# Cross attention with a top-2 expert layer on one core: straight dense half, fixed blank rows, q as products of heads and rests

## The chip, the cores and the metric

The kernel runs on one core of one Trainium2 chip. The metric is device time in microseconds (us) of one launch, the median of the runs; lower is better. The core has five engines that run side by side, each through its own list of instructions in order: PE (TensorE: matmuls and weight loads), DVE (VectorE), ACT (ScalarE), POOL (GpSimd) and SP (SyncE, here only a queue that starts DMAs). They wait for each other by semaphores.

## What is computed

64 batches of 256 tokens with 256 features, and for each batch a context of 120 rows:

```
h   = layernorm(x)
q   = h @ Wq.T + bq ;  k, v = ctx @ Wk.T + bk, ctx @ Wv.T + bv      (16 heads of 16)
att = (q @ (k.T @ v) per head) * 0.25                               (no softmax)
x1  = x + layer_norm(att + h, gamma, beta)
t   = layernorm(x1);  logits = t @ gate.T;  w, e = top2(softmax(logits))   (16 experts)
out = x1 + sum over the two choices of w * relu(t @ expert_w[e].T + expert_b[e])
```

## The kernel before

**The dense half** goes over the 64 batches in steps. In step `s` the engines work on four batches at once: batch `s` (transposes of h, k and v, q, k.T v), `p = s - 1` (attention and its residual, x1), `b = s - 2` (norm and transposes of x1, logits) and `f = s - 3` (top 2, ranks, scatter of the rows). The order on each engine is written by hand in its `step(s)`, and the engines meet through semaphores named after what is ready (`s_ht`: h transposed and copied, `s_oh`: one-hot marks ready, `s_prk`: ranks ready, `s_x1`: x1 ready). Steps up to `LEAD - 1 = 11` are written out, then a loop on every engine runs 6 times over 8 steps, and the last steps are written out again.

On PE a step is: attention of p (L673), four transposes of h (L687), k and v as three products of heads and rests (L661 to L663: a head is a value rounded to the type fp32r, a rest is what the rounding left), the first half of q (L707, plain fp32), the ranks of f (L734), transposes of x1 (L717), k.T v (L695), the second half of q (L707), logits (L729). On DVE it is: moments of x1 of b, scores of f, moments of the next x, top values (L1050), their indices (L1060), gaps (L1055, L1056), the indices cast to floats (L1067), the attention residual `att` (L1111), one-hot marks (L1071), moments of att, a shift for the next h (L1038), the ranks picked (L1096, which waits for L734), then scaling, the mask of k.T v, the softmax weights, the place of each row and x1 (L1137). POOL waits for x1 of p and then does the rest of the next context (L579), x + beta (L594), in steps 4 to 11 the rest of one eighth of the expert weights (L602), small integer work, and two scatters of 128 rows into `bins` (L621). In steps 2 to 9 PE also sums the columns of an eighth of the expert weights (L765, L767: one bf16 and two fp32 matmuls of 512 columns), and DVE folds the sum in a step later (L1150).

`settle` puts a semaphore increment of its own between a wait and the next instruction:

```
def settle(eng, passed):
    eng.sem_inc(passed, 1)
```

**The boundary.** When the last ranks are counted (`s_end`), the number of rows of every expert is known. DVE works out a table of row positions (L1231 to L1273), PE transposes it between matmuls that nobody reads (`keep_warm`, 12 ahead of the transpose and 14 behind it, L798), and `fill` (L378) writes for each of 16 experts 128 blank rows behind the expert's last row, by DMAs from DRAM to DRAM (L386): 8 started by SP, 8 by ACT. SP then reads 16 row positions into registers and starts the loads of the first rows (L488), after waiting for those DMAs (`s_padw`).

**The expert half** goes twice (first and second choice) over 144 tiles of 128 rows: load by SP, transpose by PE (L811), head by ACT (L982), rest by DVE (L1277), three products of 256 columns (L828 to L830), weighing by ACT, sum by DVE, scatter by POOL (L636). PE reads the offsets of the expert weights into registers at the top of each `multiply` (L835).

## Time and profile before

| | |
|---|---|
| time, median of 3 runs | 903.47 us (901.72 to 903.67) |
| profiled execution, own time | 903.09 us |
| its span in the trace | 901.3 us |
| PE busy | 769.8 us, 85% of the span |
| DVE busy | 664.3 us, 74% |
| ACT busy | 612.0 us, 68% |
| POOL busy | 582.3 us, 65% |

How to read it: the shares are means over stages with different limits. The dense half takes roughly the first 480 us, the boundary some 20, the expert half the rest. The span is what the trace covers; the execution's own time is 1.8 us longer.

### The profile page before, as it was taken

To read this page: it belongs to the slowest core of one execution; us is meant where nothing else is said; L and a number is where in the kernel's file an instruction comes from. 1 tells how busy PE (TensorE), PEld (TensorE's weight loads), DVE (VectorE), ACT (ScalarE), POOL (GpSimd) and SP (SyncE) were. 2 spreads that over 40 slices of the span, in tenths; PEclk is the share of its full clock that TensorE was granted. 3 is DMA by queue.
4 is the path that set the end of the run, shared out by engine and by line. 5 is a ranking of instruction groups with operands and counts; after the bars stand their busy time and mean duration, and the time that the engine had idled before them with its cause. 6 is when DMAs were issued, how large, how long until landed. Compare 5 with 4: busy or idle time off the path is not lost.

```text
span 901.3 us, 22390 instructions
## 1 busy us (share of the span) xinstructions
PE 769.8 (85%) x5549; PEld 676.3 (75%) x5550; DVE 664.3 (74%) x2291; ACT 612.0 (68%) x1722; POOL 582.3 (65%) x704
## 2 busy tenths in 40 slices
PE   4999999999999999999975878777777899777760
PEld 3777788888888888888863867677765899776760
DVE  4788999999999999999983767676763566455540
ACT  3788889999999999999970545455552565455440
POOL 3267766666666666666662577777775577777775
PEclk9999999999999999999996899999999899999995
DMA  6425556666665666666515799989985999999942
GB/s 205 153 82 160 159 180 203 219 228 200 223 228 196 231 218 200 230 215 205 190 49 169 234 306 302 307 282 311 309 295 203 323 392 352 302 290 292 310 168 76
DMA packets 138485, 207.27 MB, mean 230 GB/s; under 512 B 39718, under 2 KB 75049, under 8 KB 138185
## 3 DMA queue, kind: packets, MB, share of 16 engines
q1 hardware_dynamic: 113740, 131.56, 46.7%
q0 software_dynamic: 24448, 74.14, 22.0%
q10 hardware_dynamic: 256, 1.08, 0.4%
q8 instruction: 18, 0.29, 0.1%
q14 instruction: 23, 0.19, 0.1%
HBM read 89.91 MB, written 118.97 MB: 232 GB/s over the span
## 4 chain that ended last, share of the span: by engine, by line
PE 53%; DMA 14%; issue 12%; POOL 9%; DVE 5%; SPq 4%; ACT 1%; POOLq 0%; DVEq 0%; ACTq 0%
PE ps_q L707 12%; PE ps_att L673 7%; POOL out_rows L636 6%; PE ps_mg L729 5%; DMA row_in<-bins 5%; DMA bins<-row_in,put_at 4%; PE ps_mg L695 4%; DMA out_rows<-xh,put_at 3%; PE ps_h2t L717 3%; PE ps_kv L661 3%; PE ps_kv L663 3%; PE ps_kv L662 3%; PE ps_ht L687 3%; POOL bins L636 3%; SPq L495 2%
## 5 line engine op out<-in xcount | busy, mean ns | idle before, releaser
L636 POOL DMA_INDIRECT bins<-row_in,put_at x143 | 141.5, 990 | 68.1 <-issue 38.8
L636 POOL DMA_INDIRECT out_rows<-xh,put_at x143 | 145.0, 1014 | 56.6 <-issue 38.4
L621 POOL DMA_INDIRECT bins<-rows x128 | 128.0, 1000 | 75.9 <-POOL rows L614 50.3
L707 PE MATMUL ps_q<-h_t,wq 128*128 128x256 f32 x512 | 132.3, 381 | 0.0
L579 POOL TENSOR_TENSOR c_rest<-c_sb,c_head 128x240 fp32r<-128x240 f32 x64 | 44.3, 692 | 106.2 <-DVE x L1137 102.6
L707 PEld LDWEIGHTS ps_q<-h_t,wq 128*128 128x128 f32 x512 | 92.5, 191 | 15.5 <-ACT h_t L934 0.4
L828 PE MATMUL ps_q<-we_head,row_head 128*128 x288 | 88.4, 307 | 9.7 <-DVE row_rest L1277 9.7
L1304 DVE SCALAR_TENSOR_TENSOR row_in<-row_in 128x256 f32<-128x256 f32 x144 | 63.4, 481 | 33.8 <-ACT row_in L994 32.4
L594 POOL TENSOR_TENSOR x_beta<-xh,beta_sb 128x512 f32<-128x512 f32 x64 | 81.9, 1279 | 1.2 <-DVE x L1137 1.2
L830 PE MATMUL ps_q<-we,row_head 128*128 x288 | 81.7, 284 | 0.0
L829 PE MATMUL ps_q<-we_head,row_rest 128*128 x288 | 81.6, 283 | 0.0
L729 PEld LDWEIGHTS ps_mg<-wg_centred,h_t 128*128 128x128 f32 x512 | 64.3, 194 | 13.5 <-issue 4.9
L887 ACT ACTIVATE q_t<-ps_q,bq_sb 128x256 f32<-128x256 f32 x128 | 60.3, 471 | 20.0 <-PE ps_q L707 20.0
L673 PE MATMUL ps_att<-kvm,q_t 128*128 128x128 f32 x512 | 72.9, 285 | 0.8 <-ACT q_t L887 0.8
L1308 DVE COPY put_at<-row_in 128x2 int32<-128x2 int32 x72 | 14.3, 198 | 78.3 <-ACT xh L994 78.3
L926 ACT ACTIVATE xh<-xh,nmr,rstd 128x256 f32<-128x256 f32 x128 | 69.1, 588 | 0.2 <-DVE nmr L1038 0.2
L874 ACT ACTIVATE lnv<-st,eps 128x2 f32<-128x2 f32 x192 | 54.5, 284 | 15.2 <-DVE st L1032 15.2
L729 PE MATMUL ps_mg<-wg_centred,h_t 128*128 128x16 f32 x512 | 63.4, 256 | 1.6 <-ACT h_t L940 1.6
L828 PEld LDWEIGHTS ps_q<-we_head,row_head 128*128 128x128 f32 x288 | 55.1, 191 | 12.6 <-issue 12.5
L673 PEld LDWEIGHTS ps_att<-kvm,q_t 128*128 128x128 f32 x512 | 62.3, 192 | 1.4 <-ACT q_t L887 1.3
L911 ACT ACTIVATE rows<-x,rows 128x256 f32<-128x256 f32 x128 | 58.1, 501 | 2.1
L661 PE MATMUL ps_kv<-wkv_head,c_head 128*120 128x512 f32 x128 | 56.1, 438 | 4.0 <-DMA bkv_rows<-bkv_dram 3.8
(179 smaller groups left out, 2436.4 us busy)
## 6 DMA issues: line engine op xcount, KB each, us to landing
bins<-zeros SPq DMA_DIRECT2D x48, 768.0 KB, 4.5
row_in<-bins SPq DMA_DIRECT2D x128, 260.0 KB
row_in<-bins SPq DMA_DIRECT2D x160, 132.0 KB
xh<-in_x SPq DMA_DIRECT2D x64, 256.0 KB
c_sb<-in_ctx_t SPq DMA_DIRECT2D x64, 120.0 KB
we<-in_we_t SPq DMA_DIRECT2D x8, 512.0 KB, 6.3
bins<-row_in,put_at POOLq DMA_INDIRECT x143, 4.1
out_rows<-xh,put_at POOLq DMA_INDIRECT x143, 4.5
```

The costliest lines, as they stand in the source:

```text
L594: pool.tensor_tensor(x_beta[:, n], x_sb[:, s.buf(4)], beta_sb[:].unsqueeze(1).to_broadcast([P, NT, D]), ALU.add).then_inc(s_xb, 1)
L621: pool.indirect_dma_start(out=bins[0], in_=r[:, t, :], out_offset=bass.IndirectOffsetOnAxis(ap=r[:, t, POS_COL:POS_COL + 1].bitcast(I32), ...
L636: pool.indirect_dma_start(out=bins[1] if k == 0 else out, in_=row_in[:, t, :] if k == 0 else y[:, t, :], out_offset=bass.IndirectOffsetOnA ...
L661: pe.matmul(ps_kv[0:SC, :], head, wkv_head[:, c, :], start=(c == 0), stop=False)
L673: mm = pe.matmul(ps_att[:, t, c * P:(c + 1) * P], q_t[:, c, t, :], kvm[:, c, :], start=True, stop=True)
L707: mm = pe.matmul(ps_q[dc][:, 0:S], wq[:, c, dc * P:(dc + 1) * P], h_t[:, c, :, :], start=(c == 0), stop=(c == KC - 1))
L729: mm = pe.matmul(logits[:, t, :], h2_t[:, c, t, :], wg_centred[:, c, :], start=(c == 0), stop=(c == KC - 1))
L828: pe.matmul(o, heads, w_head, start=(c == 0), stop=False)
L829: pe.matmul(o, rests, w_head, start=False, stop=False)
L830: mm = pe.matmul(o, heads, we_rest[:, c, bass.ds(at[2 * j + t], D)], start=False, stop=(c == KC - 1))
L926: a = act.activation(h[:, b.buf(4), t, :], x_sb[:, b.buf(4), t, :], ACT.Identity, bias=nmr[:, t:t + 1], scale=rstd[:, 0, b.buf(2), t:t + 1])
L1304: at = dve.scalar_tensor_tensor(out=row_in[:, t, 0:D], in0=row_in[:, t, D:2 * D], scalar=row_in[:, t, D + S_COL:D + S_COL + 1], in1=row_in ...
```

## The change

1. **Straight code.** The loops of the dense half are written out on all engines; `Batch` loses its loop index.
2. **Fixed blank rows.** Every region of `bins[0]` keeps 128 rows at each end, which are filled with blanks in step 7 (four DMAs in place of the two that wrote `pad_rows`). An expert's rows begin behind them, and the table counts tiles so that the blank rows at the start of a region fill its last tile. `fill`, its DMAs and `pad_at` are gone. SP reads the first 4 positions ahead of the first loads and the other 12 after two pairs; PE reads its first offsets ahead of the first transposes.
3. **q in three products.** `wq` and `h` are split in heads and rests. ACT's copy of the transposed h writes `h_head`; DVE makes `h_rest` (new, 128x512 from PSUM and SBUF) between the attention residual and the one-hot marks; both halves of q and the next transposes of h wait for it (`s_hr`).
4. **Small work on DVE.** The two subtractions of the gaps are one; the one-hot marks read the integer indices; the cast of the second index goes to POOL. `settle` is gone from the dense half.
5. **Column sums.** POOL adds the two halves of an eighth of the expert weights (`we_sum`, 128x512) in steps 1 to 8, and PE sums columns with one fp32 matmul in place of two.
6. `WARM_TABLE` 12 to 16, `WARM_LOADS` 14 to 20.

```diff
-                for c in range(KC):
-                    mm = pe.matmul(ps_q[dc][:, 0:S], wq[:, c, dc * P:(dc + 1) * P], h_t[:, c, :, :],
-                                   start=(c == 0), stop=(c == KC - 1))
+                o, part = ps_q[dc][:, 0:S], slice(dc * P, (dc + 1) * P)
+                for c in range(KC):
+                    pe.matmul(o, wq_head[:, c, part], h_head[:, c, :, :], start=(c == 0), stop=False)
+                    pe.matmul(o, wq_head[:, c, part], h_rest[:, c, :, :], start=False, stop=False)
+                    mm = pe.matmul(o, wq_rest[:, c, part], h_head[:, c, :, :], start=False, stop=(c == KC - 1))
...
+            def rest_h(b):
+                dve.wait_ge(s_ht, b.times(1, 1))
+                dve.tensor_tensor(h_rest[:], ps_ht[:], h_head[:].bitcast(F32), ALU.subtract).then_inc(s_hr, 1)
...
+                    for n in pieces(s.c - 1, 1):
+                        pool.wait_ge(s_we[n], 16)
+                        if n >= 2:
+                            pool.wait_ge(s_wsum, n - 1)
+                        pool.tensor_tensor(we_sum[:, n % 2], we[:, 0, piece(n)], we[:, 1, piece(n)],
+                                           ALU.add).then_inc(s_whalf, 1)
...
-                for c in range(KC):
-                    mm = pe.matmul(ps_fold, minus_ones[:], we[:, c, piece(n)], start=False, stop=(c == KC - 1))
-                mm.then_inc(s_wsum, 1)
+                pe.matmul(ps_fold, minus_ones[:], we_sum[:, n % 2], start=False, stop=True).then_inc(s_wsum, 1)
...
-                dve.tensor_tensor(gaps[:, :, 0:E], scores[:], top[:, :, 0:1].to_broadcast([P, NT, E]), ALU.subtract)
-                dve.tensor_tensor(gaps[:, :, E], top[:, :, 1], top[:, :, 0], ALU.subtract).then_inc(s_gap, 1)
+                dve.tensor_tensor(gaps[:], scores_top[:, :, 0:E + 2], top[:, :, 0:1].to_broadcast([P, NT, E + 2]),
+                                  ALU.subtract).then_inc(s_gap, 1)
...
+                    regions = bins[0][0:SPARE, :].rearrange("(r n) d -> n r d", n=REGION)
+                    facts = pad_facts[:, 0].rearrange("p (r o) d -> p r o d", o=2)
+                    for o, ends in enumerate((regions[0:PAD], regions[REGION - PAD:REGION])):
...
-            fill(sp, 0, E // 2)
             for n in range(4):
                 sp.wait_ge(s_row[n], 32 * (NB // 4))
+            sp.wait_ge(s_init, 2 * 16 * (E // 4 + 2))
             sp.wait_ge(s_table, 1)
```

On DVE, in the middle of any step of the dense half, the program before has these rows (words in brackets are the semaphores that a row waits for):

```order
L1060 MAX_INDEX top_i<-top,scores 128x8
L1055 TENSOR_TENSOR gaps<-scores,top 128x2x16 [waits top_values_ready]
L1056 TENSOR_TENSOR gaps<-top 128x2
L1067 CAST rows<-top_i 128x2x2 [waits rows_scattered3,top_indices_ready]
L1111 TENSOR_TENSOR att<-ps_att,xh 128x512 [waits h_ready,attention_multiplied]
L1071 TENSOR_TENSOR onehot<-iota_e,rows 128x64 [waits indices_as_floats]
L1032 BN_STATS st<-att 128x6 [waits attention_residual_ready]
```

And in the changed program, at the same place:

```order
L1052 MAX_INDEX top_i<-scores_top 128x8
L1045 TENSOR_TENSOR gaps<-scores_top 128x36 [waits top_values_ready]
L1099 TENSOR_TENSOR att<-ps_att,xh 128x512 [waits h_ready,attention_multiplied]
L1103 TENSOR_TENSOR h_rest<-ps_ht,h_head 128x512 [waits h_t_heads_ready]
L1057 TENSOR_TENSOR onehot<-iota_e,top_i 128x64 [waits top_indices_ready]
L1022 BN_STATS st<-att 128x6 [waits attention_residual_ready]
```

A row of 2 elements and a cast are gone, and a subtraction of 512 elements stands between the residual and the marks. On PE, behind the products for k and v of the same step, before:

```order
L664 MATMUL ps_kv<-bkv_rows,ones_bf 120x512
L705 REGISTER_ALU [waits h_t_copied]
L707 MATMUL ps_q<-h_t,wq 128x256 [waits q_copied]
L707 MATMUL ps_q<-h_t,wq 128x256
L734 MATMUL ps_rank<-onehot,not_before 128x32 [waits rank_picked,onehot_ready]
```

and in the changed program:

```order
L653 MATMUL ps_kv<-bkv_rows,ones_bf 120x512
L697 MATMUL ps_q<-h_head,wq_head 128x256 [waits q_copied,h_t_rests_ready]
L698 MATMUL ps_q<-h_rest,wq_head 128x256
L699 MATMUL ps_q<-h_head,wq_rest 128x256
L697 MATMUL ps_q<-h_head,wq_head 128x256
L698 MATMUL ps_q<-h_rest,wq_head 128x256
L699 MATMUL ps_q<-h_head,wq_rest 128x256
L725 MATMUL ps_rank<-onehot,not_before 128x32 [waits rank_picked,onehot_ready]
```

The ranks still stand behind this half of q, which now waits for DVE's `h_rest` and not for ACT's copy. On POOL, in one of steps 4 to 8, before:

```order
L594 TENSOR_TENSOR x_beta<-xh,beta_sb 128x512 [waits x_loaded1]
L602 TENSOR_TENSOR we<-we,we_head 128x2x512 [waits weight_heads_ready]
L614 TENSOR_TENSOR rows<-rows,exps 128x2 [waits first_weight_ready]
```

and in the changed program:

```order
L574 TENSOR_TENSOR x_beta<-xh,beta_sb 128x512 [waits x_loaded3]
L584 TENSOR_TENSOR we_sum<-we 128x512 [waits weight_column_sums_ready,expert_weights_loaded6]
L589 TENSOR_TENSOR we<-we,we_head 128x2x512 [waits weight_heads_ready]
L598 TENSOR_TENSOR rows<-rows,id_step 128x2 [waits rows_scattered0]
L600 CAST rows<-top_i 128x2 [waits top_indices_ready]
L603 TENSOR_TENSOR rows<-rows,exps 128x2 [waits first_weight_ready]
```

A second large addition stands ahead of the rest of the expert weights, and a cast among the small rows.

## Rows read from the trace of the kernel before

**Rows 1.** Busy time in 100 us of the dense half, and its heading.
```profile
core 0: us, PE busy (x) PEld busy (x) DVE busy (x) ACT busy (x) POOL busy (x), PEclk, DMA share, GB/s
300.00:400.00 100.00, 100.00 (x730) 87.96 (x727) 94.66 (x390) 93.63 (x298) 62.53 (x90) 1.00 0.64 217
```

**Rows 2.** Timeline of PE in one step: start, length, engine, line.
```profile
305.61 1.03 PE L707 MATMUL ps_q<-h_t,wq 128*128 128x256 f32 x4
306.47 0.18 PE L734 MATMUL ps_rank<-onehot,not_before 128*128 128x32 bf16 x1
...
306.60 0.18 PE L734 MATMUL ps_rank<-onehot,before 128*128 128x32 bf16 x1
...
309.29 1.14 PE L673 MATMUL ps_att<-kvm,q_t 128*128 128x128 f32 x8
```

**Rows 3.** Timeline of DVE in the same step; idle time before a row in brackets.
```profile
304.47 0.09 DVE L1060 MATCH_VALUE_LOAD top_i<-top,scores 128x8 f32 x1 [0.15 <-DVE top L1050]
...
304.78 0.17 DVE L1055 TENSOR_TENSOR gaps<-scores,top 128x32 f32<-128x32 f32 x1
304.87 0.19 DVE L1056 TENSOR_TENSOR gaps<-top 128x2 f32<-128x2 f32 x1
304.98 0.15 DVE L1067 CAST rows<-top_i 128x4 f32<-128x4 uint32 x1
305.05 0.68 DVE L1111 TENSOR_TENSOR att<-ps_att,xh 128x512 f32<-128x512 f32 x1
305.65 0.21 DVE L1071 TENSOR_TENSOR onehot<-iota_e,rows 128x64 bf16<-128x64 f32 x1
...
306.81 0.23 DVE L1096 TENSOR_TENSOR picked<-ps_rank,onehot 128x64 f32<-128x64 f32 x1
```

**Rows 4.** Timeline of PE in the expert half: products of heads and rests, 256 columns.
```profile
500.19 0.28 PE L830 MATMUL ps_q<-we,row_head 128*128 x1
500.31 0.29 PE L828 MATMUL ps_q<-we_head,row_head 128*128 x1
```

**Rows 5.** Timeline of PE: the transposes of h that begin steps 9, 10, 11, 12, 63.
```profile
89.36 0.60 PE L687 MATMUL ps_ht<-ident,xh 128*128 128x128 f32 x4
...
98.16 0.60 PE L687 MATMUL ps_ht<-ident,xh 128*128 128x128 f32 x4
...
105.02 0.60 PE L687 MATMUL ps_ht<-ident,xh 128*128 128x128 f32 x4
...
113.59 0.60 PE L687 MATMUL ps_ht<-ident,xh 128*128 128x128 f32 x4
...
458.48 0.60 PE L687 MATMUL ps_ht<-ident,xh 128*128 128x128 f32 x4
```

**Rows 6.** Timelines of POOL (its step 10) and DVE (its step 11).
```profile
104.91 1.29 POOL L594 TENSOR_TENSOR x_beta<-xh,beta_sb 128x512 f32<-128x512 f32 x1
106.16 2.36 POOL L602 TENSOR_TENSOR we<-we,we_head 128x1024 fp32r<-128x1024 f32 x1
...
106.23 2.34 DVE L1055 TENSOR_TENSOR gaps<-scores,top 128x32 f32<-128x32 f32 x1
```

**Rows 7.** The boundary: timelines of PE, POOL, SP's queue and DVE.
```profile
479.09 4.58 PE L798 MATMUL ps_q<-bkv_rows,ones_bf 128*128 128x512 bf16 x12
...
481.71 0.96 POOL L621 DMA_INDIRECT bins<-rows  x1 [0.30 <-issue]
...
484.08 0.28 DVE L1273 CAST table<-ps_kv 8x128 int32<-8x128 f32 x1 [0.36 <-PE ps_kv L803]
...
490.62 8.94 SPq L488 DMA_DIRECT2D row_in<-bins  x16
...
493.46 1.09 PE L811 MATMUL ps_ht<-ident,row_in 128*128 128x128 f32 x4 [6.46 <-DMA row_in<-bins]
```

**Rows 8.** The chain that ended last, at the boundary: the blank rows.
```profile
486.29 4.16 DMA bins<-pad_rows
```

**Rows 9.** Timelines of the first product and the first scatter of the expert half.
```profile
496.41 0.58 PE L828 MATMUL ps_att<-we_head,row_head 128*128 x1 [0.79 <-DVE row_rest L1277]
...
501.94 0.95 POOL L636 DMA_INDIRECT bins<-row_in,put_at  x1 [19.27 <-DVE row_in L1304]
```

More of the change, by code:

```diff
@@ L94, in settle, with dense_steps @@
     eng.sem_inc(passed, 1)
-def dense_steps(eng, step, low, high):
-    for s in range(low, LEAD):
-        step(Batch(None, s))
-    with eng.Fori(0, LOOPS) as i:
-        for j in range(U):
-            step(Batch(i, LEAD + j))
-    for s in range(LEAD + LOOPS * U, high):
-        step(Batch(None, s))
+def dense_steps(step, low, high):
+    for s in range(low, high):
+        step(Batch(s))
 def expert_bodies(eng, body, k, peel_first=0, peel_last=0):
@@ L135, in table_reader, with read @@
     regs = [eng.alloc_register(f"column{column}_{n}") for n in range(V)]
-    def read(k, i):
+    def read(k, i, count=V):
         half = int(isinstance(i, int) and i * V >= P)
         row = (column * 2 + k) * 2 + half
-        eng.load(regs, table[row:row + 1, bass.ds(i * V - half * P, V)])
-        return [nc.snap(r, min_val=0, max_val=max_val) for r in regs]
+        low = V - count if count > V // 2 else 0
+        eng.load(regs[low:low + count], table[row:row + 1, bass.ds(i * V - half * P + low, count)])
+        return [nc.snap(r, min_val=0, max_val=max_val) for r in regs[low:low + count]]
     return read
@@ L397, in load @@
                 n = b.buf(4)
-                if b.i is not None or b.c >= 4:
+                if b.c >= 4:
                     sp.wait_ge(s_xb, (b - 4).times(1, 1))
@@ L465, in step @@
                     load(nxt)
-                if s.i is None and s.c < LEAD:
+                if s.c < LEAD:
                     prepare_experts(s.c)
-                if s.i is not None:
-                    fill_second(s, s.c - LEAD)
-            dense_steps(sp, step, 0, NB)
-            fill(sp, 0, E // 2)
+                if LEAD <= s.c < LEAD + FILLS:
+                    fill_second(s.c - LEAD)
+            dense_steps(step, 0, NB)
             for n in range(4):
                 sp.wait_ge(s_row[n], 32 * (NB // 4))
+            sp.wait_ge(s_init, 2 * 16 * (E // 4 + 2))
             sp.wait_ge(s_table, 1)
@@ L678, in transpose_h @@
                 pe.wait_ge(s_h, b.times(1, 1))
-                if b.i is not None or b.c >= 1:
-                    pe.wait_ge(s_ht, (b - 1).times(1, 1))
-                if b.i is None and b.c >= 2:
+                if b.c >= 1:
+                    pe.wait_ge(s_hr, (b - 1).times(1, 1))
+                if b.c >= 2:
                     pe.wait_ge(s_gfold, 1)
-                if b.i is None and b.c >= 3:
+                if b.c >= 3:
                     pe.wait_ge(s_fold, min(b.c - 2, WE_PIECES))
@@ L746, in rank_tokens @@
                 pe.wait_ge(s_oh, b.times(1, 1))
-                if b.i is not None or b.c >= 1:
+                if b.c >= 1:
                     close_ranks(b - 1)
@@ L834, in multiply @@
             def multiply(k, i):
-                at = offsets(k, i)
+                at = first_at if isinstance(i, int) and i == 0 else offsets(k, i)
                 for j in range(PAIRS):
@@ L848, in _ @@
                     keep_warm(ps_rank, WARM_BOUNDARY)
+                first_at = offsets(k, 0)
                 for j in range(2):
@@ L882, in copy_q @@
                 act.wait_ge(s_pq, b.times(2, dc + 1))
-                if dc == 0 and (b.i is not None or b.c >= 1):
+                if dc == 0 and (b.c >= 1):
                     act.wait_ge(s_patt, (b - 1).times(1, 1))
-                if b.i is None and b.c == 0:
+                if b.c == 0:
                     act.wait_ge(s_w[2], 32)
@@ L967, in step @@
                     context_head(s + 2)
-                for n in pieces(s.c - 3, 1) if s.i is None and s.c >= 3 else ():
+                for n in pieces(s.c - 3, 1):
                     act.wait_ge(s_fold, n + 1)
                     act.activation(we_head[:, :, piece(n)], we[:, :, piece(n)], ACT.Copy).then_inc(s_whead, 1)
-            dense_steps(act, step, -1, NB + 3)
-            fill(act, E // 2, E)
+            dense_steps(step, -1, NB + 3)
             def head_rows(k, i, j):
@@ L1204, in step @@
                     first_weights(f)
-                if f.i is None and f.c == NB - 1:
+                if f.c == NB - 1:
                     second_weights(f)
@@ L1213, in _ @@
             split(be_in[:], be_rest, be_part, 5)
-            dense_steps(dve, step, -1, NB + 3)
+            dense_steps(step, -1, NB + 3)
             steps = [0]
```

244 lines of the change are left out of this document (114 added, 130 removed).

## The prediction

> **What bounds the kernel now.** I read the stages first, then one step of the dense half on each engine, then the steps one after another, then the boundary. In the dense half PE has no idle time and DVE is busy 94.66% [rows 1]. One step of PE, from one product to the same one in the next, takes 6.70 us, and half of q takes 0.86 of it (305.61 to 306.47) [rows 2]. So PE sets the pace, but DVE is close behind: of 6.70 us it works 6.34. It idles 0.15 ahead of the index search, and it waits for the ranks: the last one ends at 306.60 + 0.18 = 306.78, and DVE picks them at 306.81 [rows 2, 3]. Hence two questions: what does PE save, and what does the work given to DVE cost there?
>
> The steps are not all alike. Step 9 takes 8.80 us (89.36 to 98.16), as the steps with column sums do, step 10 takes 6.86, and step 11 takes 8.57 without any column sum [rows 5]. There is a reason on DVE: a subtraction of 32 elements (L1055) that takes 0.17 us elsewhere takes 2.34 here, started 0.07 us behind POOL's rest of the expert weights (L602, 2.36 us), and ends with it [rows 3, 6]. An operation of DVE with both inputs in SBUF stands still while POOL works on two inputs. There is a second such hold one step later.
>
> At the boundary the table is ready at 484.36, but the first loads of rows start at 490.62, behind the blank rows, whose last DMA lands at 486.29 + 4.16 = 490.45 [rows 7, 8]. The first transposes follow at 493.46 and the first scatter of the expert half at 501.94 [rows 7, 9].
>
> **q in three products.** On PE a half of q becomes six products of 256 columns. Products of that shape start 0.12 us apart [rows 4]: 0.72 in place of 0.86, 0.28 less over a step. PE's own turn falls to about 6.42.
>
> On DVE `h_rest` is new: 512 elements, one input from PSUM and one from SBUF, like the attention residual in front of it, which takes 0.68 and lets the next one start after 0.60 [rows 3]. Taken out are the second gap subtraction (0.11, 304.87 to 304.98), the cast (0.07, 304.98 to 305.05), and with `settle` most of the 0.15 of idle time; I take 0.11 for that, an estimate, since a same-engine wait stays [rows 3]. If nothing made DVE wait, its turn would be 6.65 to 6.76 (6.34 + 0.60 less 0.18 to 0.29).
>
> But it does wait, and this is the step on which the forecast rests. Half of q on PE now waits for `h_rest`, the ranks stand behind this half, and DVE picks the ranks only three operations after it has made `h_rest` (marks, moments, shift: 1.43 us from the start of `h_rest` if nothing waits, by the spacing of the same rows now). From the start of the residual to the pick it takes 1.76 us now (305.05 to 306.81). After: 0.60 for the residual, 0.68 for `h_rest`, 0.05 for the semaphore, 0.72 for half of q, 0.31 for the ranks (306.47 to 306.78), 0.03 to the pick: 2.39 [rows 2 to 4]. The rest of DVE's turn is 6.70 - 1.76 = 4.94, less 0.29 = 4.65. The turn that closes over both engines is 7.04 us: DVE stands about 0.4 in front of the pick, PE about 0.65 in front of q. Against 6.70 that is 0.34 a step. Bounds: 6.95 if the semaphores and the first product are quicker by 0.1, 7.15 if `settle` was not what cost the 0.15. Over the 50 steps from 13 on: +17.0.
>
> **Straight code.** From step 10 to step 63 it is 360.3 us [rows 5]. Steps 10, 11 and 12 take 6.86, 8.57 and as much again for the second hold; 50 steps at 6.70 are 335.0, which leaves about 1.4 us for all ends of the loop. That is what writing it out gives: -1.4. So the long steps around the loop's entry are not the loop's. Straight steps show no stall: steps 2 to 9 are straight now and run alike. The Trainium skill says more ("Runtime: NRT & Kernel Launch", section on instruction fetch mechanics): a taken branch whose target is not at hand costs a fetch, and fetching straight code is hidden; by it the straight program costs nothing, and the traces of the straight steps agree.
>
> **Column sums, the early steps.** PE loses one of two fp32 matmuls of 512 columns, as many columns as the 0.86 of half a q: -0.86 in steps 2 to 9 [rows 2]. The pace there then goes to DVE (7.04 and the fold of more than 1 us, about 8.4) and to POOL: 62.5% of 6.70 is 4.2, with L602 6.5, with the new addition (the shape of x + beta, 1.29) 7.8, and with the idle time around its scatters close to 9.1 [rows 1, 6]. The new addition also moves L602 back by 1.25 us, onto the moment when DVE comes to its gap subtraction, and by my reckoning from these rows the two are within 0.03 us. If DVE comes first, five steps take 9.1 in place of 8.8, and with what steps 2 to 5 gain it is -1 in all. If POOL comes first, DVE is held some 2.2 us in each of five steps, which take 10.6: +9, and +7 in all. It is a tie; I put +3 in the sum and both ends in the range.
>
> The skill speaks against this part ("GPSIMD Engine Reference", Specifications): GpSimd shares its SBUF interfaces with VectorE and contends with its instructions that have two SBUF inputs. The 2.34 us of row L1055 agree; `h_rest`, with one input from PSUM, would be free of it, and the kernel's order keeps POOL's big additions behind x1.
>
> **The end of the dense half and the start.** The last three steps are chains of short operations; the cast, the gap and `settle` are on them: -0.5. At the start q follows the first k and v as now; -0.3 for its quicker products.
>
> **The boundary.** No blank rows stand ahead of the loads. What is late next is the table. Four more matmuls ahead of its transpose: the 12 took 4.58 together, 0.38 each; four of 512 columns at twice the 0.12 of 256 are about 0.9 [rows 4, 7]. That puts the table at 485.3. The last scatter is issued by 482.67 [rows 7] and should be down by about 485 to 486.8 (the blank rows took 4.16 among many [rows 8]). With 1 us for SP to read four positions the loads start at about 486.2, 4.4 earlier. PE stays at work until then, where now it idles 6.46 us ahead of the first transposes [rows 7] and does them and the first products at the lower clock, up to twice the 0.12 each. It also has its offsets already; now the first product starts 0.79 after the transposes [rows 9]. From the first transpose to the first scatter it is 8.48 us now; 12 products at the full clock give up to 1.2 of it, the transposes and the offsets as much: -2.3, an estimate. Together -6.7, with bounds -3 (the last scatter lands late, POOL sets the pace anyway) and -8. The expert half behind it is the same code, its pace set by POOL's scatters and the DMAs, so it moves as a whole.
>
> **The sum.** 903.1 for the profiled execution (0.4 below the median), -0.3 at the start, +3 in the early steps, +17.0 - 1.4 in the rest, -0.5 at the end, -6.7 at the boundary: 914.2, as a median 914.5 us.
>
> **Rivals.**
> - *DVE hides the new work.* It idles already, and the pick waits at present for PE alone. If the turn over both engines is not closed as I have it, DVE's own 6.65 to 6.76 is the step; then 50 steps give -2.5 to +3, and with -1 early, -1.4, -0.8 and -6.7 the time is 891 to 897. For it: the other rows of DVE's turn leave no other wait. Against it: `h_rest`, half of q, ranks and pick follow each other by semaphores in both programs' order. It turns the sign below a step of 6.82 to 6.90. Chance 0.12 for faster; 0.06 that the turn falls between and all is within 0.2%.
> - *The boundary gives little:* the loads wait for the last scatter or the table, and POOL's scatters take back what comes early. Then -3 or less: 918 to 921. Chance 0.07.
> - *Straight code stalls an engine:* every engine now fetches several times the instructions. A stall of 2 us every few steps makes 922 and more. No straight step shows one. Chance 0.05.
> - *The forecast,* with its own range of 907 to 920: 0.70.
>
> Faster, same and slower by 0.2% (1.8 us, about what a measurement tells from no change): 0.12, 0.06, 0.82. The range leaves out the first rival below 902 and what lies above 921.
>
> **What the profile after would show.** The transposes of h 7.04 us apart, even in steps 20 to 60; PE idle or late in front of L697 on DVE's `h_rest`, DVE idle some 0.4 in front of the ranks picked, PE's busy share below 95%. Early steps of 10.6 with the gap subtraction at 2 us, or of 9.1 without. The first loads at about 4.4 us closer behind the table, and full clock there. The prediction is wrong if steps are 6.8 or less, if many rows of DVE or PE show stalls of 2 us, or if the boundary is as long as before.

## The result and the profile after

The kernel before took 902.6 us (901.3 to 903.7, 4 runs), the changed one 923.1 us (918.3 to 925.6, 4 runs): a ratio of 1.022, 95% interval 1.018 to 1.027. It is slower, as forecast, but by 20.5 us in place of 11, and above my range (902 to 921). The profiled execution of the changed kernel took 925.58 us with a span of 923.6, so it lies 2.5 above its median.

Busy time in the same 100 us of the dense half as [rows 1]:

```profile
core 0: us, PE busy (x) PEld busy (x) DVE busy (x) ACT busy (x) POOL busy (x), PEclk, DMA share, GB/s
300.00:400.00 100.00, 95.52 (x743) 82.45 (x742) 93.66 (x351) 91.93 (x282) 60.62 (x98) 1.00 0.63 206
```

PE, which had no idle time, now has 4.5%, and no other engine is busier than before: nobody is full. That is what a turn that closes over two engines looks like. The groups of the page say where PE idles:

```profile
L697 PE MATMUL ps_q<-h_head,wq_head 128*128 128x256 f32 x256 | 85.1, 332 | 29.6 <-DVE h_rest L1103 29.6
```

The same step as [rows 2, 3], DVE first, then PE (start, length, engine, line, idle time before it):

```profile
305.63 0.24 DVE L1040 MAX8 scores_top<-scores_top 128x8 f32<-128x16 f32 x2
305.90 0.09 DVE L1052 MATCH_VALUE_LOAD top_i<-scores_top 128x8 f32 x1
...
306.21 0.18 DVE L1045 TENSOR_TENSOR gaps<-scores_top 128x36 f32<-128x36 f32 x1
306.30 0.68 DVE L1099 TENSOR_TENSOR att<-ps_att,xh 128x512 f32<-128x512 f32 x1
306.90 0.68 DVE L1103 TENSOR_TENSOR h_rest<-ps_ht,h_head 128x512 fp32r<-128x512 f32 x1
307.50 0.24 DVE L1057 TENSOR_TENSOR onehot<-iota_e,top_i 128x64 bf16<-128x64 f32 x1
...
308.80 0.23 DVE L1082 TENSOR_TENSOR picked<-ps_rank,onehot 128x64 f32<-128x64 f32 x1 [0.37 <-PE ps_rank L725]
```

```profile
307.63 0.38 PE L697 MATMUL ps_q<-h_head,wq_head 128*128 128x256 f32 x1 [0.32 <-DVE h_rest L1103]
307.86 0.28 PE L698 MATMUL ps_q<-h_rest,wq_head 128*128 128x256 f32 x1
307.97 0.28 PE L699 MATMUL ps_q<-h_head,wq_rest 128*128 128x256 f32 x1
...
308.44 0.19 PE L725 MATMUL ps_rank<-onehot,not_before 128*128 128x32 bf16 x1
...
308.58 0.18 PE L725 MATMUL ps_rank<-onehot,before 128*128 128x32 bf16 x1
```

PE waits 0.32 for the rests, DVE waits 0.37 for the ranks, each for the other once a turn. From the residual to the pick it is 2.50 us (306.30 to 308.80), where I had 2.39. The piece that I mis-sized is the first product of the six: the next one follows it by 0.23 (307.63 to 307.86), the others stand 0.11 to 0.13 apart. It isn't the wait that makes it so. The second half of q, ahead of which PE has no idle time, begins nearly alike (timeline of PE):

```profile
309.44 0.37 PE L697 MATMUL ps_q<-h_head,wq_head 128*128 128x256 f32 x1
309.65 0.28 PE L698 MATMUL ps_q<-h_rest,wq_head 128*128 128x256 f32 x1
```

The steps, by the transposes of h (steps 10, 13 and 63; the first row answers to 98.16 of [rows 5]):

```profile
99.65 0.60 PE L676 MATMUL ps_ht<-ident,xh 128*128 128x128 f32 x4
...
126.61 0.60 PE L676 MATMUL ps_ht<-ident,xh 128*128 128x128 f32 x4
...
483.69 0.60 PE L676 MATMUL ps_ht<-ident,xh 128*128 128x128 f32 x4
```

From 126.61 to 483.69 there are 50 steps of 7.14. Steps 2 to 12 are 7.7 to 8.96 long, but for two: step 9 takes 12.77 and step 12 takes 11.10. In the first of them (POOL, then DVE):

```profile
87.71 1.29 POOL L584 TENSOR_TENSOR we_sum<-we 128x512 f32<-128x512 f32 x1
88.95 2.34 POOL L589 TENSOR_TENSOR we<-we,we_head 128x1024 fp32r<-128x1024 f32 x1
```

```profile
88.25 0.17 DVE L1052 FIND_INDEX8 top_i<-scores_top 128x8 uint32<-128x16 f32 x1
88.34 3.06 DVE L1045 TENSOR_TENSOR gaps<-scores_top 128x36 f32<-128x36 f32 x1
91.32 0.68 DVE L1099 TENSOR_TENSOR att<-ps_att,xh 128x512 f32<-128x512 f32 x1
```

An operation of 0.18 us takes 3.06: it meets POOL's addition (L584) and stands through the rest of the weights (L589) as well. I call this a hold. In the early steps of 8.96 us it stands only for the end of L584, gets in ahead of L589 and takes 0.43 or less; there it is the one-hot marks, also from SBUF to SBUF, that stand until L589 ends, for 1.22 in place of 0.24 (step 8; L589 from 79.73 to 82.08):

```profile
80.94 1.22 DVE L1057 TENSOR_TENSOR onehot<-iota_e,top_i 128x64 bf16<-128x64 f32 x1
```

The hold of step 9 makes DVE only 1.9 us later than a step of 8.96 (3.06 less 0.18, less the 1.0 that the marks no longer stand). The other 1.9 is PE's: it idles 3.56 ahead of q, and then runs at half the clock. The window behind the wait (its clock is the 0.50 near the end of the line):

```profile
93.10:96.30 3.20, 3.20 (x22) 3.11 (x21) 1.78 (x7) 1.47 (x4) 1.36 (x2) 0.50 0.26 90
```

The variant with the rests of h ahead of the attention has the same hold. In the third set of experiments below its clock stayed up:

```profile
90.40:93.00 2.60, 2.10 (x22) 2.06 (x23) 2.60 (x8) 0.94 (x4) 1.52 (x4) 1.00 0.31 69
```

In the second set it fell:

```profile
92.60:97.00 4.40, 4.40 (x25) 4.31 (x26) 3.24 (x13) 1.49 (x5) 1.97 (x2) 0.50 0.30 83
```

Where the clock falls to 0.50 (1.2 GHz), DVE waits for PE's ranks, k.T v and column sum.

The boundary, beside [rows 7, 9]: PE, DVE, SP's queue, PE, POOL.

```profile
503.85 6.39 PE L787 MATMUL ps_q<-bkv_rows,ones_bf 128*128 128x512 bf16 x16
...
510.45 0.28 DVE L1259 CAST table<-ps_kv 8x128 int32<-8x128 f32 x1 [2.23 <-PE ps_kv L792]
...
514.52 0.66 PE L800 MATMUL ps_ht<-ident,row_in 128*128 128x128 f32 x4
...
520.98 0.97 POOL L625 DMA_INDIRECT bins<-row_in,put_at  x1 [13.56 <-DVE row_in L1290]
```

```profile
511.65 9.59 SPq L468 DMA_DIRECT2D row_in<-bins  x16
```

The last pick of ranks ends at 503.69 (478.94 before). From there to the table it is 6.76 us (5.14 before), to the first loads 7.96 (11.68), to the first scatter 17.29 (23.00). The loads come 3.7 earlier, and the way from the first transposes to the first scatter is 6.46 in place of 8.48. The clock of both sides of the table, by windows:

```profile
503.90:509.30 5.40, 5.40 (x16) 1.86 (x14) 3.84 (x27) 0.00 (x0) 1.96 (x2) 0.50 0.14 50
510.50:514.00 3.50, 3.50 (x18) 1.55 (x16) 0.23 (x1) 0.00 (x0) 0.00 (x0) 1.00 0.28 79
```

The 16 matmuls ahead of the table run at a granted clock of 0.50 (1.2 GHz), after a tail in which PE was busy for 4.2 of 7.7 us (496.0 to 503.7) at that clock already, and stand 0.43 apart; the 20 behind it run at 1.00 and stand 0.22 apart.

Where the 22.3 us between the two spans lie: -0.8 at the start, +5.3 in steps 1 to 13, +20.7 in steps 13 to 63, -0.5 from there to the last pick, -5.7 to the first scatter, and +3.3 in the expert half. The last is the same code, and it takes 394.8 to 401.9 us in the profiles of the last three sets of experiments, 402.6 here and 399.4 in the kernel before: spread between executions, by all that these show.

### The profile page after: what moved, and what is told of

The parts are those of the page before. It is cut to its first block, busy times and chain, and to the rows that moved or that the text cites. A ratio compares the mean times of both kernels' runs of the same rounds, so it can differ in the third digit from the quotient of the medians.

```text
span 923.6 us, 21777 instructions
## 1 busy us (share of the span) xinstructions
PE 772.2 (84%) x5799; PEld 679.6 (74%) x5800; DVE 693.7 (75%) x2225; ACT 626.5 (68%) x1723; POOL 602.7 (65%) x776
## 4 chain that ended last, share of the span: by engine, by line
DVE 35%; issue 22%; PE 17%; DMA 10%; POOL 9%; SPq 4%; ACT 2%; DVEq 0%; POOLq 0%; ACTq 0%
POOL out_rows L625 6%; DVE x L1129 6%; DVE scaled L1116 5%; DVE h_rest L1103 4%; DMA bins<-row_in,put_at 4%; DVE att L1099 4%; DMA row_in<-bins 4%; POOL bins L625 3%; DVE st L1022 3%; PE ps_q L697 3%; DVE top_i L1052 2%; DMA out_rows<-xh,put_at 2%; DVE scores_top L1040 2%; SPq L475 2%; DVE gaps L1045 1%
## 5 line engine op out<-in xcount | busy, mean ns | idle before, releaser
L625 POOL DMA_INDIRECT bins<-row_in,put_at x143 | 143.5, 1004 | 62.9 <-issue 38.6
L697 PE MATMUL ps_q<-h_head,wq_head 128*128 128x256 f32 x256 | 85.1, 332 | 29.6 <-DVE h_rest L1103 29.6
L697 PEld LDWEIGHTS ps_q<-h_head,wq_head 128*128 128x128 f32 x256 | 49.2, 192 | 59.4 <-DVE h_rest L1103 59.1
L698 PE MATMUL ps_q<-h_rest,wq_head 128*128 128x256 f32 x256 | 72.4, 283 | 0.0
L699 PE MATMUL ps_q<-h_head,wq_rest 128*128 128x256 f32 x256 | 72.2, 282 | 0.0
L879 ACT ACTIVATE q_t<-ps_q,bq_sb 128x256 f32<-128x256 f32 x128 | 60.4, 472 | 13.5 <-PE ps_q L699 13.5
L720 PE MATMUL ps_mg<-wg_centred,h_t 128*128 128x16 f32 x512 | 67.4, 264 | 1.5 <-ACT h_t L932 1.4
```

Of the source, the lines that this page charges most:

```text
L625: pool.indirect_dma_start(out=bins[1] if k == 0 else out, in_=row_in[:, t, :] if k == 0 else y[:, t, :], out_offset=bass.IndirectOffsetOnA ...
L697: pe.matmul(o, wq_head[:, c, part], h_head[:, c, :, :], start=(c == 0), stop=False)
L698: pe.matmul(o, wq_head[:, c, part], h_rest[:, c, :, :], start=False, stop=False)
L699: mm = pe.matmul(o, wq_rest[:, c, part], h_head[:, c, :, :], start=False, stop=(c == KC - 1))
L720: mm = pe.matmul(logits[:, t, :], h2_t[:, c, t, :], wg_centred[:, c, :], start=(c == 0), stop=(c == KC - 1))
```

## The experiments

Edits are against the changed kernel unless said otherwise. They come in five sets. Each set had its own chip with its own runs of the kernel before, so a ratio is comparable within a set. On the chips of the first two sets the kernel before took 1056 us in place of 902, and every kernel was slower in nearly all steps from 13 on and in the expert half; absolute times in the expectations of these two sets were made for 902.

**First set.** Three variants of the changed kernel, and one of the kernel before.

`e1`: the rests of h ahead of the attention.

```diff
-                if p.exists():
-                    add_attention(p)
                 if s.exists():
...
                     rest_h(s)
+                if p.exists():
+                    add_attention(p)
```

> The changed kernel with one thing moved: DVE makes h_rest ahead of the attention residual in place of behind it. Nothing is left out. Theory A (the loss is a turn over two engines: residual 0.60, h_rest 0.68, half of q, ranks, then the pick, 7.14 us a step): h_rest comes 0.6 us earlier, the wait ahead of the pick goes, and a step falls to what DVE or PE needs by itself, 6.65 to 6.75 us. Over the 50 steps that is 19 to 25 us, and 2 to 9 more in the early steps: about 893 to 901 against 923. Theory B (DVE simply has too much work, 0.6 us more a step): the order changes nothing, the step stays at 7.1 and the time within 3 us of 923. Theory C (straight code is slow to fetch): likewise no change.

`e3`: q as before the change (`h_t`, `wq`, one fp32 product; no `h_rest`), all else of the change kept.

```diff
-                    pe.matmul(o, wq_head[:, c, part], h_head[:, c, :, :], start=(c == 0), stop=False)
-                    pe.matmul(o, wq_head[:, c, part], h_rest[:, c, :, :], start=False, stop=False)
-                    mm = pe.matmul(o, wq_rest[:, c, part], h_head[:, c, :, :], start=False, stop=(c == KC - 1))
+                    mm = pe.matmul(o, wq[:, c, part], h_t[:, c, :, :], start=(c == 0), stop=(c == KC - 1))
```

> The changed kernel with q as before: plain fp32 matmuls from one copy of h, no heads and rests of Wq and h, no h_rest on DVE. Nothing is left out. Theory A: a step falls to PE's 6.70 us, the early steps and the boundary keep their gains: 891 to 899. Theory B (too much work on DVE) says the same here. Theory C (straight code): a step stays above 7.0 us and the time above 915.

`e5`: the column sums again as two fp32 matmuls on PE, POOL's `we_sum` taken out.

> The changed kernel with the column sums as before: two fp32 matmuls on PE, no addition of the two halves on POOL. Nothing is left out. If the two gap subtractions of 3.06 and 2.86 us in the early steps come from POOL's additions in a row, at least the first of them goes and the time falls by 2 to 6 us. Rival: they belong to the rest of the expert weights alone, as the two holds of 2.3 us before did, and the early steps only get PE's 0.86 us back eight times: the time rises by 0 to 4 us.

`e4`: the kernel before, with its dense half written out straight and nothing else of the change.

> The kernel before with its dense half written out, and nothing else changed. Theory A: 1 to 2 us faster (the ends of six loops), no stalls. Theory C (fetching straight code stalls the engines): several us slower.

| kernel | us | ratio to before, 95% |
|---|---|---|
| rests first | 1046.3 | 0.992, 0.989 to 0.995 |
| q plain | 1042.2 | 0.987, 0.983 to 0.990 |
| sums on PE | 1062.5 | 1.006, 1.003 to 1.008 |
| before, straight | 1046.3 | 0.991, 0.987 to 0.994 |

The order is as the turn through the rests wants it, but the steady steps are 7.5 us and more, the straight version of before too (7.52), so this chip doesn't tell 7.14 from 6.70, and the changed kernel itself was not in this set. Straight code costs nothing: it took 9.6 us less than before, more than the 1 to 2 expected, and why so much was not found (1.8 in the third set). With the sums on PE the first of the two holds shrinks to 0.90 and the second stays (2.82), but the early steps are 9.6 to 9.7 us, where the changed kernel has 8.96 in the next set, and the ratio is 1.006 against 1.000 there. So the rival was right, and the sums on POOL are no loss.

**Second set**, to have the changed kernel itself beside its variants.

> The changed kernel unchanged, as the mark for the others of this call. 2% slower than the kernel before if this chip runs the dense half as the first one did (steps of 7.14 us against 6.70); about level with it if the steady steps are 7.5 us for both, as in the four runs before.

> h_rest ahead of the attention residual, nothing else, once more, since in the run before all steady steps stood at 7.5 us for another reason, with the mask of k.T v waiting 0.7 us each step. Theory A (turn over two engines): steps of 6.65 to 6.75 us, 893 to 901 us, 2 to 3% faster than the changed kernel. Theory B (too much work on DVE): like the changed kernel.

> q as before in the changed kernel, once more for the same reason. Theory A: steps of 6.70 us, 891 to 899 us. If a step stays above 7.0 us, q is not where the time goes.

`f4` has the rests first and `WARM_TABLE` 10 in place of 16.

> h_rest ahead of the residual, and 10 matmuls in place of 16 ahead of the transpose of the table. In the profile of the changed kernel the 16 take 6.2 us and the table's transpose waits 2 us for them. Theory: 1.5 to 2.5 us faster than the kernel with h_rest first alone. Rival: the scatter of the last rows lands no sooner, or PE's clock falls for want of work, and nothing is gained.

Measured against before: the changed kernel 1.000 (0.998 to 1.003, 1056.8 us), rests first 0.990 (0.985 to 0.995), q plain 0.988 (0.983 to 0.993), rests first with 10 matmuls 0.988 (0.983 to 0.994). So on this chip the change costs nothing, and both ways of freeing q from the wait give 1%, where 2 to 3% were expected; the 10 matmuls are not told from the 16. What made the steps long there? I put it down to the blank rows that SP writes to the second bins: one step near the end took 7.14 in the changed kernel and 6.7 in the others, and I took it for a step without them (step 62). The windows don't bear that out. It is step 60, in which the last of them are written, and the steps 61 and 62 behind it, with hardly any transfers left, are long again (the changed kernel, 500.04 is the start of step 61):

```profile
492.90:500.04 7.14, 6.82 (x55) 5.89 (x54) 6.67 (x26) 6.51 (x21) 4.23 (x7) 1.00 0.58 191
500.04:507.70 7.66, 6.77 (x55) 5.83 (x54) 6.78 (x27) 6.44 (x21) 4.45 (x9) 1.00 0.14 50
```

In the straight version of before step 62 takes 7.52 as well, at 40 GB/s. The short step 60 also has POOL's second scatter issued some 2 us later than in the steps around it; whether that matters was not tried, and in the straight version of before step 61 is short (6.81) without it. The next set was made for the theory of the blank rows.

**Third set**: three of these kernels and the straight version of before, with these blank rows written two portions a step in steps 36 to 59, so that steps 14 to 35 are without them.

```diff
-                if LEAD <= s.c < LEAD + FILLS:
-                    fill_second(s.c - LEAD)
+                half = LEAD + FILLS // 2
+                if half <= s.c < LEAD + FILLS:
+                    fill_second(2 * (s.c - half))
+                    fill_second(2 * (s.c - half) + 1)
```

> The changed kernel with the blank rows of the second bins written two portions a step in steps 36 to 59 instead of one a step in steps 12 to 59 (same bytes, same rows, same order of everything else). Steps 14 to 35 then run without those transfers. My theory (the closed turn of VectorE and TensorE through the rests of h sets the step, and the transfers only lay something on top on this chip) expects 7.14 us a step there, as in the profile of the changed kernel and in its step 62 here (7.14), instead of the 7.6 to 7.85 of the run before. The rival (the slower steps on this chip are of the chip, whatever the transfers) expects 7.6 to 7.85 there as well. For steps 36 to 59 both leave 7.8 or more; the time as a whole 1045 to 1060.

> The same late blank rows, and VectorE makes the rests of h ahead of adding the attention. My theory: with the 0.60 us of add_attention out of the turn the step is set by what set it before the change, so 6.70 to 6.75 us in steps 14 to 35, 0.4 less than the kernel with the late rows alone, about 9 us over those 22 steps and some 15 to 20 over the dense half. The rival (the turn is paced by VectorE's whole work or by PE's own, not by what stands ahead of the rests) expects 7.1 in both.

> The same late blank rows, and q as one plain fp32 product on TensorE as before the change (no heads, no rests), everything else of the change in place. My theory: 6.70 us in steps 14 to 35, as before the change and as with the rests first, so that three products of heads and rests bring nothing in a steady step even when they no longer cost: TensorE's 0.28 us a step are not on the path that sets it. The rival (a faster q shows once the wait for the rests is gone) expects this kernel 0.1 to 0.3 us a step behind the one with the rests first.

> The kernel before with its dense half written out straight and the same late blank rows (nothing else of the change): the yardstick of the other three. Both theories expect 6.69 to 6.71 us in steps 14 to 35, as in the profile of the kernel before; if it is 7.5 as with the blank rows spread over steps 12 to 59, the slower steps on this chip are not from those transfers and the comparison of the steady steps has to be made otherwise.

This chip was one like that of the prediction (before: 901.2 us, 25 runs):

| late blank rows and | us | ratio to before, 95% | steady step |
|---|---|---|---|
| nothing else | 919.3 | 1.019, 1.013 to 1.025 | 7.14 |
| rests first | 897.4 | 0.996, 0.994 to 0.999 | 6.72 |
| q plain | 894.8 | 0.994, 0.991 to 0.996 | 6.70 |
| before, straight | 899.3 | 0.998, 0.996 to 1.000 | 6.70 |

One exchange of two operations on DVE is worth 22 us (919.3 to 897.4). The rests-first kernel in steps with twice the blank rows, by windows:

```profile
290.00:430.00 140.00, 139.88 (x1104) 122.88 (x1104) 138.12 (x520) 133.27 (x418) 92.22 (x147) 1.00 1.02 334
```

At 334 GB/s the steps are as long as without the transfers (6.72), so here they lay nothing on top; what makes the steps long on the other two chips was not found. And DVE has no idle time in a steady step. From one subtraction to the next pick (rests first, timeline of DVE, a step without blank rows):

```profile
204.74 0.18 DVE L1047 TENSOR_TENSOR gaps<-scores_top 128x36 f32<-128x36 f32 x1
204.91 0.69 DVE L1105 TENSOR_TENSOR h_rest<-ps_ht,h_head 128x512 fp32r<-128x512 f32 x1
205.51 0.68 DVE L1101 TENSOR_TENSOR att<-ps_att,xh 128x512 f32<-128x512 f32 x1
...
206.92 0.22 DVE L1084 TENSOR_TENSOR picked<-ps_rank,onehot 128x64 f32<-128x64 f32 x1
```

The pick has no wait before it. 6.72 is DVE's own work, inside the 6.65 to 6.76 that I had for a DVE that never waits. With q plain it is PE's own, 6.70. So the cheaper q never shows in a steady step: what PE saves, DVE spends. And PE saves less than I had: half of q takes 0.81 with the rests first too, where the plain one takes 0.86, and PE is busy for 139.88 of the 140 us.

**Fourth set**, for the early steps and the table. `h5`: the gap subtraction as two operations with one tensor input.

```diff
-                dve.tensor_tensor(gaps[:], scores_top[:, :, 0:E + 2], top[:, :, 0:1].to_broadcast([P, NT, E + 2]),
-                                  ALU.subtract).then_inc(s_gap, 1)
+                for t in range(NT):
+                    i = dve.tensor_scalar(gaps[:, t, :], scores_top[:, t, 0:E + 2], top[:, t, 0:1], None, ALU.subtract)
+                i.then_inc(s_gap, 1)
```

> The changed kernel with one edit: VectorE's gap subtraction is two operations with one tensor input and a scalar per partition each, in place of one with two tensor inputs in SBUF. My theory (the holds of 3.06 and 2.86 us are that operation standing still while GpSimd works on two SBUF inputs): the new operations take 0.1 to 0.2 us everywhere, the two steps of 12.77 and 11.10 fall to about 9 and 8, so 6 to 8 us less over steps 1 to 13; steady steps get longer by the second operation, at most 0.1 us (7.2), or +4 us over the dense half. In all 0 to 6 us below the changed kernel (917 to 923 where that has 923). The rival (the long steps come from something else, such as GpSimd's own work, and the hold only lies in it) expects the same two long steps with the wait moved to another operation.

`h1` is the same with the rests first.

> The rests of h ahead of the attention and the gap subtraction with one SBUF tensor input. By my theory the holds (3.06 and 2.87 us in the kernel with the rests first and late blank rows) are gone and steps 9 to 12 lose some 5 us; VectorE sets the steady step with its own work (6.72, no idle time in it), so the second small operation adds its 0.08 to 0.1 to every step: 6.80 to 6.82, +5 us. In all about the time of the rests first alone, 897 to 901 where the kernel before has 901. The rival expects long steps as before and 6.8 us in the steady ones, about 904.

`h3` has q plain and `WARM_TABLE` 10; `h4` adds the one-input subtraction to it.

> q plain as before the change, and 10 matmuls ahead of the transpose of the table in place of 16. The timeline of the changed kernel shows those 16 start 0.42 us apart (at the lower clock) and the table's cast waiting 2.23 us for the transpose behind them. My theory: 6 fewer are worth 6 x 0.42 = 2.5 us, of which at most 2.2 us show before the table's own computation ends last: first loads of the expert half 2 us earlier after the last pick than in the kernel with 16, unless the last scatter has not landed. In all 893 where the kernel before has 901. The rival (the loads wait for the last scatter of the dense half, not for the table) expects the first loads at the same place, 0 us gained.

> q plain, 10 matmuls ahead of the table, and the gap subtraction with one SBUF tensor input. TensorE sets the steady step here (6.70) and VectorE has 0.5 us to spare, so the second small operation is hidden, and the holds of the gap subtraction (2.2, 1.7 and 2.9 us in the kernel with q plain) go: by my theory 3 to 6 us less than q plain with 10 matmuls, 887 to 890 where the kernel before has 901, the best of all. The rival expects no gain over q plain with 10 matmuls.

Measured, with before at 902.0 us: `h5` 944.3 (ratio 1.046, 1.042 to 1.051), `h1` 912.4 (1.012, 1.008 to 1.015), `h3` 893.4 (0.990, 0.987 to 0.994), `h4` 894.7 (0.992, 0.989 to 0.995). My expectation of the holds fell: the one-input form is held too, and more often. `h5`, timelines of POOL and DVE:

```profile
77.66 2.36 POOL L589 TENSOR_TENSOR we<-we,we_head 128x1024 fp32r<-128x1024 f32 x1
```

```profile
77.51 0.17 DVE L1053 FIND_INDEX8 top_i<-scores_top 128x8 uint32<-128x16 f32 x1
77.60 2.46 DVE L1046 TENSOR_SCALAR gaps<-scores_top 128x18 f32<-128x18 f32 x2
79.97 0.68 DVE L1100 TENSOR_TENSOR att<-ps_att,xh 128x512 f32<-128x512 f32 x1
```

The first of the two gets through, the second meets L589 at 77.66 and ends with it. Eight early steps have one of 1.2 to 2.5 us, one step takes 13.58 us, and steps 1 to 13 grow by another 13.5 us. `h1` has the steady step that was expected (6.81), and the same kind of long early steps (up to 13.03). The steady step is 7.31: the pair takes 0.27 instead of 0.09 on the path ahead of the rests, and 0.17 of these 0.18 show. In `h4`, where PE sets the steady step, the same 0.18 cost nothing (6.70). Its early steps are 9.53 in place of 8.95 in `h3`, and these 0.58 are not the price of its hold of 2.48: in `h3` the marks stand in its place (1.81 for 0.21), so DVE loses 0.6 in all. The table in `h3` is ready 5.12 us after the last pick instead of 5.95 in `g3`, and the first scatter follows 15.81 instead of 16.48 after it: 6 matmuls fewer are worth 0.7 by this, where 2 were expected: in `g3` the table waits only 1.20 for its transpose (2.23 in the changed kernel's profile), and in `h3` 0.36, so the table's own computation ends last. The two profiles are of different chips, and the times (893.4 and 894.8) don't tell the difference.

**Fifth set**: the subtraction as it is, but behind the rests of h.

```diff
                     top_indices(f)
-                    score_gaps(f)
...
                 if f.exists():
+                    score_gaps(f)
                     mark_experts(f)
```

> The changed kernel with one move: VectorE's gap subtraction stands behind the attention and the rests of h instead of ahead of them. My theory: a hold then stands behind the rests of h, TensorE goes on with q, and the attention and the rests (1.2 us) are done while GpSimd still adds: the steps of 12.77 and 11.10 fall by at least 1.2 each, to 11.5 and 9.9 or less. And the 0.09 us of the subtraction leave the path from the pick through the rests of h to the next pick, into the 0.37 us that VectorE waits there: 7.05 us in the steady steps, 4.5 us over the dense half. In all 7 to 9 us below the changed kernel, 914 to 916 where that has 923. The rival (a hold costs its length wherever it stands, and the step is VectorE's sum of work) expects 12.8, 11.1 and 7.14 again.

`i2` is `h3` with the same move.

> The best kernel so far (q plain, 10 matmuls ahead of the table; 893.4 where the kernel before has 902.0) with the gap subtraction behind the attention. TensorE sets the steady step, 6.70 in any case. My theory: the attention (0.6 us) goes ahead of the holds, so the steps with holds (9.3, 7.9 and 8.7) lose up to 0.6 each, 1 to 2 us in all: 891 to 893. The rival expects the same 893.4 or more, since the subtraction now comes 0.6 us later and may meet GpSimd's 2.3 us addition in every one of steps 4 to 9 (0.6 us each, +3 us), as the two small operations did.

`i1` took 908.8 us (907.9 to 912.9; ratio to before 1.009, 1.006 to 1.012), `i2` 891.4 (0.990, 0.984 to 0.996). That is more than expected of `i1`: steady steps of 7.04, and no step above 9.1 among steps 1 to 12. Of `i2` it is as expected, but its ratio is that of `h3`; by the two profiles steps 1 to 13 are 1.8 us shorter. At the place of the 3.06 us hold (`i1`, DVE):

```profile
88.80 0.67 DVE L1099 TENSOR_TENSOR att<-ps_att,xh 128x512 f32<-128x512 f32 x1
89.38 0.68 DVE L1103 TENSOR_TENSOR h_rest<-ps_ht,h_head 128x512 fp32r<-128x512 f32 x1
89.98 1.56 DVE L1045 TENSOR_TENSOR gaps<-scores_top 128x36 f32<-128x36 f32 x1
```

POOL's L589 runs from 89.12 to 91.48 there. The residual and the rests, with an input from PSUM, run in 0.67 and 0.68 under it as ever; only the subtraction stands, and PE is at q meanwhile; its clock stays at 1.00 through the step (90.20 to 96.40). In a steady step the pick's wait is 0.28 where it was 0.37:

```profile
306.25 0.22 DVE L1082 TENSOR_TENSOR picked<-ps_rank,onehot 128x64 f32<-128x64 f32 x1 [0.28 <-PE ps_rank L725]
```

## Why the prediction was right or wrong

- **The closed turn** was right as a mechanism. Everything that the forecast rests on shows: PE late in front of L697 (0.32, where I had 0.65), DVE late in front of the pick (0.37, where I had 0.4). Three edits move it as it says: 0.60 off the path gives 6.72, where DVE's own work takes over; 0.09 off gives 7.04; 0.18 more gives 7.31. What was off is the sum that was built on it.
- **Its size** was the largest error, and the step that failed is the term "0.72 for half of q". The rest of DVE's turn is 7.14 - 2.50 = 4.64 (I had 4.65), residual and rests with the semaphore 1.33 (1.33), the ranks and the way to the pick 0.36 (0.34), but half of q 0.81 (0.72). I took the steady pitch of [rows 4] for all six products, but the first one needs 0.23. Over 50 steps 0.44 in place of 0.34 makes +22.0 instead of +17.0. The trace of the kernel before had such a product two rows ahead of [rows 4], with no idle time in front of it (timeline of PE):

```profile
499.84 0.39 PE L828 MATMUL ps_q<-we_head,row_head 128*128 x1
500.07 0.28 PE L829 MATMUL ps_q<-we_head,row_rest 128*128 x1
```

  The same term makes PE's own turn too short: 6.42 rests on saving 0.28 a step, and the halves measured (0.81, and about 0.79 for the second) leave some 0.12, an estimate from the rows above.

- **Straight code**: -1.4 forecast, -1.3 measured (22.0 - 20.7). The agreement is in part luck: of the 1.4 in the kernel before, about 1.0 lies at five ends of the loop (steps of 6.81 and 6.78 around each) and 0.4 in step 61 (7.12), which isn't the loop's and is 7.28 in the changed kernel. There is no stall of instruction fetch in any timeline that I read, though the two instruction queues moved 0.97 MB where they had 0.48. That rival is out.
- **Early steps**: +3 forecast for a tie, +5.3 measured. Neither of my cases came, five holds or none: the order between the two engines was settled anew in each step, and twice to the bad side. What failed is the price: I gave a hold 1.8 us a step (10.6 for 8.8), and it cost 3.8 in step 9 (12.77 against 8.96). My price had DVE's delay, and not what PE does behind it. PE idled 3.56 us ahead of q and its clock fell to 0.50. With the rests first, where they stand behind the held subtraction too, a hold of 3.06 cost 1.7 in the third set (10.64 against 8.95), with a clock of 1.00 after 2.98 of idle time, and one of 3.02 cost 4.4 in the second (13.32 against 8.96), with a clock of 0.50 after 2.92. So the difference goes with the clock, and not with the order of the two operations; why it fell in one and not in the other is not shown. The Trainium skill ("GPSIMD Engine Reference", Specifications) names instructions with two SBUF inputs, and those in a 2-port mode, as the ones that contend. The trace agrees for the first kind; for the one-input subtraction, held as well, no run shows in which mode it ran.
- **The end of the dense half**: -0.5 and -0.5. **The start**: -0.3, measured -0.8.
- **The boundary**: -6.7 forecast, -5.7 measured. The 16 matmuls put the table 1.6 later, where I had 0.9 for four more at twice 0.12: with 512 columns they stand 0.43 apart at the lower clock, and [rows 7] already had the twelve at 0.38 each. First loads 3.7 earlier (I had 4.4), transposes to scatter 2.0 less (2.3).
- **The sum**, made against the profiled execution: 914.2 forecast; 925.6 less the 3.3 of the expert half are 922.3 measured. Of these 8.1 us 5.1 are in steps 13 to 63, 2.3 in the early steps, 1.0 at the boundary, -0.5 at the start, and 0.2 lie outside the spans. The range failed as well: the steady step is inside the bounds that I gave it (6.95 to 7.15), and the early steps came out under the +7 that I gave them, but the two bounds together lie at 924 (914.5 + 50 x 0.11 + 4), and the range ended at 921.

The rival that DVE hides the new work was wrong in this order of its operations, and right with the two exchanged.

What I would keep of the change is the rest of it: q plain, 10 matmuls ahead of the table and the subtraction behind the residual take 891.4 us, 1.0% (0.4 to 1.6) below the kernel before, and no kernel here is measured faster; `h3`, without the last of these, is not told from it (0.990 both).

## What to carry to other kernels

Cutting the work of the busiest engine by adding a hand-over to the next busiest is to be priced as a turn: follow the new wait round to itself, and sum what stands on it, each engine's queue included. Then look at what stands directly ahead of the new operation in its engine's order, since an operation that isn't on the turn (the residual, the subtraction) can often go behind it for nothing; here that exchange was worth 22 us. Price a short group of products by a whole group in the trace, the first one included, and not by the pitch in its middle. And where a new wait leaves PE idle for long (2.9 to 3.6 us here), price the work behind it at both clocks.

## What the runs showed of the hardware

- The first product of a group of heads and rests (256 columns, granted clock 1.00) keeps the next one off for 0.20 to 0.23 us instead of 0.12, with a wait in front of it (307.63) or without (309.44; 499.84 in the kernel before). Why is not shown.
- A short operation of DVE from SBUF to SBUF, with one or with two tensor inputs, stands still while POOL adds two SBUF tensors, and may stand through two additions in a row (3.06 us); one that gets in ahead of an addition can leave the next one to stand (marks of 1.22 us); the index search, the statistics and operations with an input from PSUM take their usual time under the same additions.
- After 3.56 us without a product, PE's clock fell to 0.50 for 3.2 us and more, and after 2.98 us it stayed at 1.00 in one run and fell after 2.92 in another.
- Matmuls meant to keep the clock up can be at their dearest behind a thinly used stretch of PE: the 16 took 6.39 us in the changed kernel, at a granted clock of 0.50 up to 509.3, and 5.39 in `g1`, where the mean clock from 503.9 to 509.0 was 0.77.
- In the first two sets every version ran some 14 to 17% slower, with most steps from 13 on at 7.5 us and more, with the blank rows written beside them and without, and with a slower expert half; in the third set twice the writes at once changed nothing in a step. This was seen, not explained.
